# One core, four layers: the mixer stage with fixed bias columns, a reordered tail, the gate product in another bank, and z rounded ahead of the gate's silu

## What is computed

```python
x = L0_attn_hidden_states                                   # 1 x 1024 x 512, fp32
x = x + _L0_attn_ref(_layernorm(x), ...)                    # the mixer (SSM), 8 groups, 64 heads
x = x + _L0_ffn_ref(_layernorm(x), ...)                     # gated MLP, 4-bit weights
x = x + _L1_attn_ref(_layernorm(x), ...)                    # attention within each position
x = x + _L1_ffn_ref(_layernorm(x), ...)                     # linear with a 2-of-8 low-rank part
# the mixer:
proj = hidden @ in_proj_w.T                                 # gate, hbc (x, B, C), dt
xBC  = silu(conv(hbc, 4 taps) + conv_bias)
state = state * dA_t + dtx_t * B_t ;  y_t = C_t . state     # scan over 1024 positions
y  = y + x * D
yn = y * rsqrt(mean(y*y over the group's 512)) * norm_weight * silu(gate)
out = yn @ out_proj_w.T
```

## Time and profile before

| | |
|---|---|
| median of 3 runs | 1276.28 us (1273.55 to 1276.47) |
| the profiled execution, its own time | 1275.21 us |
| its span, first to last instruction | 1273.4 us |
| TensorE busy | 1195.9 us, 94% |
| VectorE busy | 927.3 us, 73% |
| ScalarE busy | 829.5 us, 65% |
| GpSimd busy | 655.2 us, 51% |
| mean granted TensorE clock | 0.978 |

### The profile page before, as it was taken

One profiled execution on the slowest core, in us unless ns is written; L12 is line 12 of the kernel. 1 busy time (PEld: TensorE's weight loads), 2 busy tenths in 40 slices (PEclk: granted clock), 3 DMA queues, 4 the chain that ended last, 5 costly groups with the idle time before them and its releaser, 6 DMA issues. The chain is left out here.

```text
span 1273.4 us, 22145 instructions
## 1 busy us (share of the span) xinstructions
PE 1195.9 (94%) x6342; PEld 940.0 (74%) x6342; DVE 927.3 (73%) x1728; ACT 829.5 (65%) x1522; POOL 655.2 (51%) x710
## 2 busy tenths in 40 slices
PE   6999999999999999999999999998679999789976
PEld 5777777777777777777777777777567777677754
DVE  5796688669677866967786696788666556479985
ACT  6788878788877877887787888777633333222220
POOL 5056547646654764665476466545743434333330
PEclk9999999999999999999999999999889999999996
DMA  4223133222313312331332233122304232312100
GB/s 166 91 92 104 55 108 109 67 84 93 106 50 108 107 66 83 93 105 50 108 107 66 83 95 103 50 80 75 90 26 141 87 97 72 94 46 62 40 9 25
DMA packets 80038, 104.81 MB, mean 82 GB/s; under 512 B 8662, under 2 KB 48926, under 8 KB 79708
## 3 DMA queue, kind: packets, MB, share of 16 engines
q1 hardware_dynamic: 79964, 104.00, 26.0%
HBM read 96.89 MB, written 7.09 MB: 82 GB/s over the span
## 5 line engine op out<-in xcount | busy, mean ns | idle before, releaser
L755 DVE SCALAR_TENSOR_TENSOR conv<-p_tile,conv_taps,conv 128x511 f32<-128x511 f32 x186 | 139.0, 748 | 24.0 <-ACT conv L588 4.9
L605 ACT ACTIVATE em<-em,cum_tok 128x128 f32<-128x128 f32 x512 | 156.1, 389 | 0.0
L864 DVE TENSOR_TENSOR em<-em,p_gb 128x512 f32<-128x512 f32 x128 | 82.1, 683 | 88.3 <-ACT em L641 88.1
L527 POOL TENSOR_TENSOR squares<-squares 128x256 f32<-128x256 f32 x64 | 46.9, 732 | 139.3 <-ACT squares L669 139.3
L91 PE MATMUL p_tile<-xn_hi,wc_hi 128*128 128x512 f32 x248 | 103.0, 415 | 3.7 <-ACT gate_second L628 2.4
L593 ACT ACTIVATE xbc<-conv 128x512 f32<-128x512 f32 x96 | 60.8, 633 | 66.6 <-DVE conv L763 43.6
L91 PE MATMUL p_d<-wr_hi,zt_hi 128*128 128x512 f32 x236 | 93.8, 397 | 5.8 <-ACT zt_hi L598 5.8
L91 PE MATMUL p_tile<-xn_lo,wc_hi 128*128 128x512 f32 x248 | 97.4, 393 | 0.0
L755 DVE SCALAR_TENSOR_TENSOR conv<-p_gate,conv_taps,conv 128x511 f32<-128x511 f32 (+2 forms) x90 | 67.0, 744 | 37.3 <-ACT conv L588 32.7
L495 POOL TENSOR_TENSOR x_w<-xs,head_g 128x512 f32<-128x512 f32 x56 | 58.5, 1045 | 68.0 <-ACT xs L637 66.6
L91 PE MATMUL p_d<-wr_lo,zt_hi 128*128 128x512 f32 x236 | 93.0, 394 | 0.0
(11 more groups left out here) (406 smaller groups left out, 3568.4 us busy)
## 6 DMA issues: line engine op xcount, KB each, us to landing
em<-cum_rows SPq DMA_DIRECT2D x64, 512.0 KB, 4.0
w_raw<-w SPq DMA_DIRECT2D x108, 256.0 KB, 4.4
e_cum<-e_cum_rows SPq DMA_DIRECT2D x112, 128.0 KB, 2.9
q_words<-q SPq DMA_DIRECT2D x33, 256.0 KB, 2.7
h_ring<-h_lo_rows SPq DMA_DIRECT2D x6, 704.0 KB, 4.8
h_lo_rows<-h_rest SPq DMA_DIRECT2D x11, 256.0 KB, 2.0
x_res<-x SPq DMA_DIRECT2D x8, 256.0 KB, 4.3
out<-out_t SPq DMA_DIRECT2D x8, 256.0 KB, 2.0
```

The lines of the kernel that those rows point to most:

```text
L605: made = act.activation(steps, steps, ACT.Relu, scale=-1.0, bias=cum_tok[:, c, bass.ds(g * HG + h, 1)])
L755: ve.scalar_tensor_tensor(out=conv[:, s, sh:], in0=p[:, 0:HALF - sh], scalar=conv_w[:, bass.ds(g, 1), j, tap], in1=conv[:, s, sh:], op0=AL ...
L864: ve.tensor_tensor(m, m, gm.unsqueeze(1).broadcast_to([P, HG // 2, P]), ALU.mult)\
```

## The change

Five things are changed, in the mixer:

1. **Fixed columns.** VectorE copies the group's columns of `cum_tok` into a buffer `cum_g` of fixed addresses: chunks 1 to 7 at the group's start, chunk 0 of the next group behind it. ScalarE's decay steps read their bias from there.
2. **The bank.** The gate's product of chunks with c mod 4 below 2 goes to `p_d1`. The tiles j = 2 and j = 4 now wait for the taps of the tile that was in `p_tile`; the gate's product waits for the variance (`s_v`) that reads the column of sums in `p_d1`; and the next column of sums (in chunks 1, 2, 5 and 6) waits for the gate's silu.
3. **ScalarE's order.** The gate's silu stands behind z in every chunk.
4. **The tail** (last group, chunks 4 to 7). TensorE makes the sums and the output product ahead of the new state; VectorE makes the variance ahead of `em` and the residual ahead of the state; GpSimd makes `x_w` and `g_rstd` ahead of `state_dec`; ScalarE makes the decay steps ahead of `row_round`.
5. **Small work.** GpSimd converts the small operands in chunk 1 and clears the three buffers in chunk 4.

```diff
     def gate_bank(c):
-        return p_tile if c % CH < 2 else p_gate
+        return p_d1 if c % CH < 2 else p_gate
...
 # GpSimd
-                if 0 < c < NC - 1:
-                    pool.wait_ge(s_stu, st)
-                    pool.tensor_tensor(by_head(state_dec[:]), by_head(state[:]), heads(ETOT, c), ALU.mult)\
-                        .then_inc(s_std, 1)
+                if 0 < c < NC - 1 and not (last and c >= CH):
+                    decay_state(c, st)
...
                     pool.tensor_tensor(by_head(x_w[:]), by_head(xs[:]), heads(DTW, c), ALU.mult)\
                         .then_inc(s_xw, 1)
+                if last and c >= CH:
+                    norm(n - 1, (c - 1) % 2)
+                    if c < NC - 1:
+                        decay_state(c, st)
...
-                if last and c == CH - 1:
-                    small_operands()
...
+                if last and c == 1:
+                    small_operands()
+                if last and c == CH:
                     pool.wait_ge(s_z, (G - 1) * NC + CH)
                     up.zeros(pool)
...
 # ScalarE
             act.wait_ge(s_dl[c % 2], 16 * (g * (NC // 2) + c // 2 + 1))
+            wait(act, s_head, g * 6 if c == 0 else g * 6 + 5)
             for h in range(HG):
                 steps = em[:, c % 2, h * P:(h + 1) * P]
-                made = act.activation(steps, steps, ACT.Relu, scale=-1.0, bias=cum_tok[:, c, bass.ds(g * HG + h, 1)])
+                made = act.activation(steps, steps, ACT.Relu, scale=-1.0, bias=cum_g[:, c, h:h + 1])
...
+                if last and CH <= c < NC - 1:
+                    decay_steps(g, c + 1)
                 for k in rows_in(last, c):
                     row_round(k)
...
-                if c == 0:
-                    gate_silu(CH + n, made[1], made[2], gate_bank(c))
...
-                if made and 0 < c % CH < 2 or made and c == CH:
-                    gate_silu(CH + n, made[1], made[2], gate_bank(c))
                 z_round(n, y_bank(last, c))
-                if made and c % CH >= 2:
+                if made:
                     gate_silu(CH + n, made[1], made[2], gate_bank(c))
...
 # VectorE
+            ve.wait_ge(s_e, g * (3 * NC) + 1)
+            ve.tensor_scalar(cum_g[:, 1:, :], cum_tok[:, 1:, bass.ds(g * HG, HG)], 1.0, None, ALU.mult)\
+                .then_inc(s_head, 1)
+            if not last:
+                ve.tensor_scalar(cum_g[:, 0, :], cum_tok[:, 0, bass.ds(g * HG + HG, HG)], 1.0, None, ALU.mult)\
+                    .then_inc(s_head, 1)
...
 # TensorE, conv_tile
-            elif j in (1, 2, 4):
+            elif j == 1:
                 wait(pe, s_sg, made)
             else:
-                wait(pe, s_tap, tapped(g, hf, {3: 2}.get(j, j)))
+                wait(pe, s_tap, tapped(g, hf, {2: 1, 3: 2, 4: 3}.get(j, j)))
...
                 if c % CH < 2:
-                    pe.wait_ge(s_tap, tapped(tg, hf, 2 * j) + TAPPED[hf])
+                    wait(pe, s_v, n)
...
                     wait(pe, s_v, n - 1)
+                    if c % CH in (1, 2):
+                        pe.wait_ge(s_sg, CH + n)
                     sum_rows(n - 1, ss_bank(last, c))
```

More of the change, by code:

```diff
@@ L146, in mixer @@
     cum_tok = sb("cum_tok", [P, NC, H])
+    cum_g = sb("cum_g", [P, NC, HG])
     head_g = sb("head_g", [P, 3, NC, HG])
@@ L490, in group @@
                 if c == 0:
-                    pool.wait_ge(s_head, 4 * (g + 1))
+                    pool.wait_ge(s_head, g * 6 + 4)
                 pool.wait_ge(s_xs, n + 1)
@@ L515, in group @@
                     pool.tensor_tensor(y[:], y[:], x_d[:], ALU.add).then_inc(s_txd, 1)
-                if last and c >= CH:
-                    norm(n - 1, (c - 1) % 2)
-                if last and c == CH + 1:
+                if last and c == 1:
+                    small_operands()
+                if last and c == CH:
                     pool.wait_ge(s_z, (G - 1) * NC + CH)
@@ L522, in group, with decay_state @@
                     rstd_of(c - 1)
+        def decay_state(c, st):
+            pool.wait_ge(s_stu, st)
+            pool.tensor_tensor(by_head(state_dec[:]), by_head(state[:]), heads(ETOT, c), ALU.mult)\
+                .then_inc(s_std, 1)
         def sum_squares(m):
@@ L660, in group @@
                 made = gate_tile(g, last, c)
-                if c == 0:
-                    gate_silu(CH + n, made[1], made[2], gate_bank(c))
[L663 to L666, removed]
+                if not (last and c >= CH):
+                    decay_steps(*((g, c + 1) if c < NC - 1 else (g + 1, 0)))
                 act.wait_ge(s_y, n + 1)
@@ L728, in scalar @@
         gate_silu(3, 3, 0)
-        act.wait_ge(dt_ve, 11)
+        act.wait_ge(dt_ve, 12)
         decay_steps(0, 0)
@@ L859, in group @@
                     tile_taps(*tile, range(3, TAPPED[tile[3]]))
+                if tail:
+                    variance(n - 1, (c - 1) % 2, ss_bank(last, c))
                 ve.wait_ge(s_gm, 2 * (n + 1))
@@ L876, in group @@
                     ve.tensor_tensor(y[:], p_in[:], e_cum[:], ALU.mult).then_inc(s_t, 1)
+                if tail:
+                    residual(n - 1, c - 1, out_bank(last, c))
                 if c < NC - 1:
@@ L891, in group @@
                 if tail:
-                    variance(n - 1, (c - 1) % 2, ss_bank(last, c))
-                    residual(n - 1, c - 1, out_bank(last, c))
                     row_stats(c - 1)
@@ L987, in vector @@
         ve.tensor_copy(by_half(cum_tok), transposed(p_d0)).then_inc(dt_ve, 1)
+        ve.wait_ge(dt_ve, 11)
+        ve.tensor_copy(cum_g[:, 0, :], cum_tok[:, 0, 0:HG]).then_inc(dt_ve, 1)
         for j in range(2, TILES):
@@ L992, in vector @@
         ve.tensor_tensor(dtw_t[:], dtw_t[:], dt_t[:], ALU.mult).then_inc(dt_ve, 1)
-        ve.wait_ge(dt_ve, 12)
+        ve.wait_ge(dt_ve, 13)
         group(0, False)
@@ L1116, in group @@
                     mm.then_inc(s_inter, 1)
+                if tail:
+                    pe.wait_ge(s_res, n - 1)
+                    pe.wait_ge(s_v, n - 1)
+                    sum_rows(n - 1, ss_bank(last, c))
+                    pe.wait_ge(s_sg, LAST + 1)
+                    out_product(n - 1, out_bank(last, c))
                 if c < NC - 1:
@@ L1125, in group @@
                     conv_tile(*tile, made=CH + n)
[L1127 to L1132, removed]
                 for k in rows_in(last, c):
```

## The result

| | before | after |
|---|---|---|
| median of the runs shown with the result, us | 1276.38 (1273.55 to 1279.6, 4 runs) | 1259.82 (1257.41 to 1264.28, 4 runs) |
| ratio, 95% interval | | 0.9873 (0.9855 to 0.989) |
| span of the profiled execution, us | 1273.4 | 1256.4 |

The time lies in the predicted range, 6.8 us above the predicted 1253. But the gain does not come from where the prediction had it, as the page, the waits and a table of chunks show.

What follows compares the result with a forecast made beforehand. TensorE was taken as the bound, busy 1195.9 of 1273.4 us, with other waits in the tail. Terms 9.0 + 1.2 + 4 + 9.4 - 0.3 = 23.3 us, from 1276.3 to 1253 us; range 1243 to 1267.

Steps and rivals of the forecast that it cites:

- Term 1: Chunks 2, 5 and 6: projection tiles no longer wait for the gate's silu in their bank, 9.0 us gained.
- The cover: TensorE reaches the column of sums 24 matmuls, over 5 us, later, so its new wait for the gate's silu costs nothing.
- Term 2: Chunk 0: TensorE's 0.67 us wait for taps becomes one for the variance; 0 gained, 0.1 us a group lost at worst.
- Term 3: Chunk 0 of groups 0, 1 and 7: silu behind z, so z is rounded without that wait; 1.2 us gained.
- Term 4: Five loop restarts: ScalarE restarts freely, VectorE gets a pause of the same kind; 0.8 us gained each, 4 us.
- "3.68": ScalarE's pause in us at a loop restart in the kernel before, taken as the length of VectorE's new pause.
- its slower rival: Restarts: VectorE's pause beyond some 3.6 us stops GpSimd and TensorE; slower from 7.4 us on, 1294 us at 11; chance 0.07.
- The prediction's other case: Restarts: neither ScalarE nor VectorE pauses, 9 us gained in place of 4, 1248 us; chance 0.15.
- The test named ahead: Loop passes: the forecast is wrong where they are not at least 1 us shorter than 111.
- Term 5: Last group, chunks 4 to 7: sums and output product run while `x_w` is made; 9.4 us gained.
- the floor of "GpSimd at about 9.4 us": Tail chunks: GpSimd, the busiest engine, was taken as the next bound at about 9.4 us a chunk.
- the rival that the tail gives nothing: Tail: VectorE takes the variance's wait ahead of `em`, chunks end as before, 1262 us; chance 0.12.

Runs made afterwards that it cites:

- e1: The kernel before with the bank part alone (gate products of chunks 0, 1, 4 and 5 in p_d1, with their waits): 1267.44 us, ratio 0.993 to 0.994 not split; ratio 0.994.
- e8: The kernel after with ScalarE's old order of the gate's silu against the decay steps, squares and z: 1266.07 us, ratio 0.9924.
- e7: e5 with 16 more waits on ScalarE ahead of everything, which move its loop body by 8 instructions: 1255.63 us, ratio 0.9833.
- e9: The kernel before with the fixed columns alone, and VectorE's three head copies made as one: 1270.3 us, ratio 0.9952.
- e5: The kernel after with one head copy of VectorE in place of three (dt, dtw and etot in one tensor): 1243.84 us, ratio 0.9745.
- e2: The kernel before with the fixed columns alone, and the copy ahead of the first group: 1283.0 us, ratio 1.0054.
- e3: The kernel before with the tail's order and the small work alone: 1263.59 us, ratio 0.991.
- e6: The kernel after with 64 one-column memsets of VectorE ahead of the loop, nothing in the loop changed: 1249.34 us, ratio 0.979.
- e10: e5 with four one-column memsets of VectorE ahead of its first data: 1256.84 us, ratio 0.9846.

## Why the prediction was right in its sum, and where it failed

The sum is right in part by luck: two terms that were priced too low made up for some of the loss in one whose sign was wrong. The time lies in the range for that reason, and not because the restarts did what was forecast.

**Term 1, the bank: right.** 9.0 us priced; the chunks concerned give 9.2 in after, the run with the bank alone 7.9 by the medians. The cover held: no wait for the gate's silu is left.

**Term 2, the bank in chunk 0: right** at nothing (e1).

**Term 3, ScalarE's order: mis-sized.** 1.2 us priced, 2.6 by the chunks of before and after (0.1 in group 0, 0.8 in each of groups 1 and 7, 0.8 in chunk 3 of the last group), 6 by e8's medians with the doubts said there. The list of waits in the prediction leaves out the 0.6 us for the sums in that chunk 3, and where no restart precedes z's place was worth 0.8 us, not the 0.4 of the wait's row. That the rest is what stopping and starting TensorE costs was not shown. The step "behind the five restarts z itself is made by VectorE, so the order gives nothing there" holds only while an engine pauses: chunk 1 takes 16.3 us with either order in e1 and e7, and in after the order gives nothing in sum. Where neither engine pauses it decides: 15.88 us without it (e9), 15.07 with it (e5), in every restart. Terms 3 and 4 were priced apart, and there they work only together.

**Term 4, the fixed columns: the mechanism right, the size and the sign wrong.** The forecast was that ScalarE is relieved and VectorE takes the pause, and both happened. The failed number is "3.68": VectorE's pause was taken at ScalarE's size and was 28.6 / 5 = 5.7 us, so `x_w` came 2.2 us later in the pass and not 0.3. So what the prediction gave as its slower rival, that each microsecond beyond 3.6 stops GpSimd and TensorE, was at work without turning the sum: (5.7 - 3.6) x 5 = 10.5 us, and the waits for `x_w` at the five restarts are 12.4 - 1.2 = 11.2. On top came the clock (below). In place of a gain of 4 us the columns alone cost 7.6 (e2), and in after chunks 0 and 1 of the five restarts cost 8.3. The prediction's other case, that neither engine pauses, was put at 9 us gained against before; it is 5.9 with the columns alone (e9), and with all other parts in place e5 is 16 us faster than after. The test named ahead came out against the forecast: loop passes in after take 110.8 to 112.1 us, where 110 was asked.

**Term 5, the tail: right in kind, too low.** 9.4 us priced, 13.0 by the chunks (4.0, 2.1, 3.6 and 3.3 in place of 2.5, 1.6, 2.7 and 2.6), 11.8 by e3's medians with an interval of 9 to 14. In chunk 4 up to 1.5 us of it are the better clock of this trace. What is sure is chunks 5 and 6, 8.9 and 8.5 us in all seven traces with the new tail. The step that failed there is the floor of "GpSimd at about 9.4 us". In the earlier trace rows GpSimd's 9.46 us of chunk 5 hold three memsets (1.27, 0.53 and 0.53 us), and the change moves them to chunk 4, where GpSimd has time. The windows of after's chunks 4 and 5 (columns as above):

```profile
883.38:896.66 13.28, 9.37 (x58) 7.42 (x57) 7.67 (x24) 10.28 (x21) 9.69 (x13) 0.87 0.20 62
896.66:905.55 8.89, 7.81 (x58) 6.25 (x57) 7.93 (x18) 8.38 (x19) 7.96 (x10) 1.00 0.37 106
```

GpSimd is busy for 7.96 us, and a chunk takes 8.9, with ScalarE at 8.38. VectorE did not become the bound, and the rival that the tail gives nothing falls.

In sum, by the traces of before and after: 12.3 us too much at the restarts (a loss of 8.3 against a gain of 4), and 5.0 too little in the order (2.6 against 1.2) and the tail (13.0 against 9.4). The bank gave 0.4 more than priced, 0.3 of it in chunk 0 of group 0. Ahead of group 0, where the copy was to cost 0.3, after is 0.3 ahead.

The Trainium skill (Runtime: NRT & Kernel Launch, section "Instruction fetch mechanics") gave the reason to expect a pause on VectorE and no length for it. The case agrees with it in kind: where the branch's target isn't held, the engine stands, with loads beside it. The sizes differ. The Trainium skill's section has blocks of 16 KiB, 256 instructions; a load here is 8.2 KB, one for some 125 instructions, and 380 instructions, nearly three such blocks, restart without a load. Two blocks of 256 with the same edges for both engines, every second one of those above, do not fit: either VectorE's body 324 to 708 or ScalarE's 297 to 583 would lie within them, and both pause.

## What to carry to other kernels

In a loop that the engines branch through, look at each engine's first instruction behind the branch: idle time there without a releaser, with instruction loads beside it, was code being fetched in this kernel, and where the body lies decides it as much as its length. Price such a pause by who waits for that engine first. Up to the slack of that work it costs what the rest of the engine's chain loses (1.2 to 1.9 us a restart for pauses of 3.4 to 4.0 us: e9 against before, e6 and e7 against e5). Behind the slack each further microsecond comes on top. Before adding a few instructions to an engine whose loop restarts freely, count how far its body is from the edge.

## What I had not expected of the hardware

- Four one-column memsets ahead of everything cost 13 us of 1244 (e10), and 64 gain 10 of 1260 (e6).
- The clock takes part. Two windows behind two restarts of after, at the same place of the pass:

```profile
281.30:284.90 3.60, 3.60 (x10) 2.62 (x9) 3.17 (x9) 0.96 (x2) 1.25 (x2) 0.53 0.00 0
393.00:396.60 3.60, 3.60 (x22) 2.59 (x22) 3.19 (x8) 1.30 (x2) 1.28 (x2) 1.00 0.00 0
```

In the first the granted clock is 0.53, nearly all at the lower level, 1.2 GHz, and TensorE starts 10 matmuls in place of 22. It had stood for 2.46 us for `x_w`; ahead of the second, 2.12:

```profile
280.61 1.24 PE L1143 MATMUL p_x<-x_w,b_tok 128*128 128x512 f32 x2 [2.46 <-POOL x_w L493]
...
392.33 1.12 PE L1143 MATMUL p_x<-x_w,b_tok 128*128 128x512 f32 x2 [2.12 <-POOL x_w L493]
```

Three of the five restarts went this way. Their chunk 0 takes 18.2 to 18.4 us, the other two 16.5, so the low clock adds some 1.8 us to a wait of 2.3. The pass gets only 1.0 to 1.2 us longer by it (111.9 to 112.1 against 110.9), since chunk 1 then takes 15.07 us in place of 15.8. The waits ahead of the low clock were 2.2 to 2.5 us and the others 2.1, too close for a rule. In e5, without the wait, the clock of a pass is 1.00.
